# Layer 0's experts on the picked rows, and layer 1's window attention written out step by step

## The chip, the cores and the metric

The kernel runs on one core of one Trainium2 chip. The metric is the device time of one execution in microseconds (us), as the median of repeated runs. The profile is that of one execution on the same core. TensorE is PE in it (PEld its weight loads), VectorE is DVE, ScalarE is ACT, GpSimd is POOL, SyncE is SP.

## The reference

Two batches of 4096 tokens of width 256 pass through two layers, each with an attention and an expert part, in f32. The change is in layer 0's expert part and in layer 1's attention. Layer 0's expert part, cut:

```python
logits = einsum('bsd,ed->bse', x, gate_w) + gate_b      # 32 experts
probs = softmax(logits, axis=-2)                        # over the 4096 tokens
vals, idx = top_k(probs over tokens, 8)                 # each expert picks 8 tokens
tok = take_along_axis(x, idx)                           # (b, 8, 32, 256)
merged = einsum('bked,bke->bed', tok, vals)             # one row per expert
h = gelu([merged, 1] @ w1[e])                           # 257 x 1024 per expert
o = [h, 1] @ w2[e]                                      # 1025 x 256 per expert
out = zeros_like(x).at[idx].add(o * vals)               # added to the picked tokens
x = x + gb * out
```

Its input is the layer norm of x, times (1 + cb) plus sb. At most 512 of the 8192 rows of x change, and each expert's weights, 2 MB, are read for two rows (one of each batch). Layer 1's attention gives each token 16 of the scores over the 64 before it, and two more.

## The kernel before, in words

The program is a chain of stages with a barrier of all engines between them. A stage starts its semaphores, runs one instruction stream per engine and clears them. Four stages matter here.

**Token choice** (`build_token_choice`, tiles `tc_`). SP loads `x` in four chunks of 2048 tokens (2 MB each) and, behind the first, 14 small tables (identity, gate weights, modulation), on which DVE, PE and ACT wait (`consts`). DVE normalizes a chunk (`normalize`, L1634) into `h`, PE turns it and makes the logits (`turn`, `route`), ACT copies them into `probs` [32 experts, 4096 tokens] per batch. Per batch then: DVE's maximum (`peak`, L1648), ACT's exponential (L1602), and in `choose` four passes of DVE over 32x4096: the scaling (L1654), the best 8 (L1656), taking these out (L1658) and the difference (L1660), which leaves `chosen`, a dense matrix with 8 entries other than zero per expert. PE turns `chosen` (L1554) and multiplies it with `h` (L1563); `merge` makes `merged`.

**Experts** (`build_experts`, `ex_`). Eight rounds of four experts. SP loads the 4 MB of w1 and the 4 MB of w2 of a round into one of two sets of buffers; the load for round r + 2 waits for `up_done` and `down_done` of round r. PE's work in a round is `up` (L1768), the turning (L1776) and `down` (L1785), with two copies and a bias on DVE and gelu on ACT between. After the last round eight small transfers turn `outs` into `expert_out`, and L1822 adds the bias of w2.

**Scatter** (`build_scatter`, `sc_`). A loop reads all 8192 rows of `x1` again, multiplies `chosen` with `expert_out` on PE (L1883), gates (L1895) and adds (L1897) on DVE, and writes `x2`.

**Window attention** (`build_window_attention`, `wa_`). 16 steps of 512 tokens (four tiles). `run_steps` writes out the first two and the last two; the 12 between run as a hardware loop of two steps a turn, on all five engines. In a step PE and DVE work turn by turn: scores and the best 16 of a tile, probabilities, the products with the values, the sum into `x`; further on in the step DVE scales `h` of step it + 2 (`normalize`, with the modulation L2311 and L2313) and takes the values of step it + 1 (L2320). POOL makes a product of 128x1024 (L2282) and four small ones (L2288) per step.

Of the kernel before, what the change touches and what calls it, by code (L numbers as in the profile page):

```python
# [1443 lines left out]
def build_token_choice(nc, d, merged, chosen):  # L1444
# [5 lines left out]
    WAYS = P // EXPERTS  # L1450
    with ExitStack() as ctx:
        sb = lambda name, shape: ctx.enter_context(nc.sbuf_tensor("tc_" + name, shape, F32))
# [11 lines left out]
        h = sb("h", [P, GROUPS, T, DIM])  # L1464
        x = [sb(f"x{i}", [P, T, DIM]) for i in both]
# [8 lines left out]
        chosen_T = sb("chosen_T", [P, GROUPS_PER_BATCH * T, EXPERTS])  # L1474
        part = sb("part", [P, DIM])
# [3 lines left out]
        ch_ps = [ps(f"ch_ps{i}", [P, 512]) for i in both]  # L1479
        part_ps = ps("part_ps", [P, 512])  # L1480
# [3 lines left out]
        routed, logits_out, peak_ready, exp_done, chosen_ready, chosen_turned, chosen_copied, part_done, part_ready, summed, merged_out = map(sem, (  # L1484
            "routed", "logits_out", "peak_ready", "exp_done", "chosen_ready", "chosen_turned", "chosen_copied", "part_done", "part_ready", "summed", "merged_out"))
        x_in = [sem(f"x_in{i}") for i in both]
        CONSTS = 16 * (4 + BATCH + 4 * BATCH)

        sem.start()
        with nc.Block() as block:  # L1490
            @block.sync
            def _(sync):
                def load_x(g):
                    if g >= 2:
                        sync.wait_ge(h_ready, at((g - 1) * QUADS))
                    sync.dma_start(flat(x[g % 2][:, :, :]), chunk_rows(d["x1"], g)).then_inc(x_in[g % 2], 16)
# [3 lines left out]
                sync.dma_start(stack[:, :], d["stack"]).then_inc(consts, 16)  # L1500
                sync.dma_start(gate_w[:, :, :], d["gate0_wT"].rearrange("(k p) n -> p k n", p=P)).then_inc(consts, 16)
# [11 lines left out]
            def _(pe):  # L1513
# [6 lines left out]
                def turn(q, half):  # L1520
                    n = q * 2 + half
                    pe.wait_ge(h_ready, at(q + 1))
                    if n >= 2:
                        pe.wait_ge(hT_ready, at(n - 1))
                    for k in range(HALVES):
                        for t in range(2):
                            mm = pe.transpose(tr_ps[n % 2][:, (k * 2 + t) * P:(k * 2 + t + 1) * P], h[:, q // QUADS, q % QUADS * Q + half * 2 + t, k * P:(k + 1) * P], ident[:, :])
                    mm.then_inc(turned, 1)
# [18 lines left out]
                for b in range(BATCH):  # L1547
                    pe.wait_ge(chosen_ready, at(b + 1))
                    for gg in range(GROUPS_PER_BATCH):
                        n = b * GROUPS_PER_BATCH + gg  # L1550
                        if n >= 2:
                            pe.wait_ge(chosen_copied, at(n - 1))
                        for j in range(T):
                            mm = pe.transpose(ch_ps[n % 2][:, j * EXPERTS:(j + 1) * EXPERTS],  # L1554
                                              chosen[:, b, gg * P * T + j:(gg + 1) * P * T:T], ident[0:EXPERTS, 0:EXPERTS])
                        mm.then_inc(chosen_turned, 1)
                    tiles = GROUPS_PER_BATCH * T
                    pe.wait_ge(chosen_copied, at((b + 1) * GROUPS_PER_BATCH))
                    if b > 0:
                        pe.wait_ge(part_ready, at(b))  # L1560
                    for n in range(tiles):
                        way = n % WAYS
                        mm = pe.matmul(part_ps[way * EXPERTS:(way + 1) * EXPERTS, 0:DIM], chosen_T[:, n, :], h[:, b * GROUPS_PER_BATCH + n // T, n % T, :],  # L1563
                                       start=(n < WAYS), stop=(n >= tiles - WAYS), skip_group_check=True)
                    mm.then_inc(part_done, 1)

                    pe.wait_ge(part_ready, at(b + 1))
                    pe.wait_ge(weights_ready, at(1))
                    if b > 0:
                        pe.wait_ge(merged_out, at(b * HALVES))  # L1570
                    for k in range(HALVES):
                        pe.matmul(mg_ps[:, 0, k, :], part[:, k * P:(k + 1) * P], stack[:, :], start=True, stop=True, skip_group_check=True)
                        mm = pe.matmul(mg_ps[:, 1, k, :], shift[:, b, k * P:(k + 1) * P], weight_of[:, b, :], start=True, stop=True, skip_group_check=True)
                    mm.then_inc(summed, 1)

            @block.scalar
            def _(act):
                act.wait_ge(consts, at(CONSTS))
# [21 lines left out]
                def exponents(b):  # L1600
                    act.wait_ge(peak_ready, at(b + 1))
# [3 lines left out]
                for q in range(ALL_QUADS + 1):  # L1605
# [6 lines left out]
                    if q == ALL_QUADS - QUADS:  # L1612
                        exponents(0)
                exponents(1)
                for n in range(GROUPS):
                    act.wait_ge(chosen_turned, at(n + 1))
                    if n >= GROUPS_PER_BATCH:
                        act.wait_ge(part_done, at(n // GROUPS_PER_BATCH))
                    i = n % GROUPS_PER_BATCH
                    act.copy(chosen_T[:, i * T:(i + 1) * T, :].rearrange("p t e -> p (t e)"), ch_ps[n % 2][:, :]).then_inc(chosen_copied, 1)  # L1620
# [320 lines left out]
def is_first(it):  # L1941

    return isinstance(it, int) and it == 0
# [1133 lines left out]
```

## Time and profile before

| what | value |
|---|---|
| median of 3 runs | 3483.39 us (3483.12 to 3486.39) |
| profiled execution, its own time | 3495.82 us |
| its span | 3493.6 us |
| granted TensorE clock over the span | 0.77 |
| PE, DVE, ACT, POOL busy | 73%, 59%, 38%, 25% of the span |

The span is what the profile covers; 2.2 us of the execution's time lie around it. Times in rows count from the span's start. The four stages stand at these places: token choice from 1556, experts from 1694, scatter from 1875, window attention from 1967 to 2761. Behind it the slots and layer 1's experts follow, which the change doesn't touch.

### The profile page before, as it was taken

The page shows a single profiled execution, that of the slowest core. Times are in us where ns is not written, and L with a number is a line of the kernel's source. Part 1 is how long each engine was busy: PE and PEld are TensorE (multiplying, and loading weights), DVE is VectorE, ACT ScalarE, POOL GpSimd, SP SyncE. Part 2 cuts the span into 40 slices and gives each one's busy share as a digit, 9 for nine tenths or more (in the row PEclk, how much of TensorE's full clock was granted, in tenths as well). Part 3 has the DMA queues.
Part 4 walks back from the last instruction along what each step waited for, and adds up shares of the span by engine and source line. Part 5 has one row for each costly group of instructions (what it writes and reads, how often), then busy time and mean ns, then how long its engine had stood idle before and what let it go on. Part 6 is the DMA issues. An engine that isn't in the chain of part 4 may idle for free. (4 is left out here: it accounts for less than half of the span.)

```text
span 3493.6 us, 109335 instructions
## 1 busy us (share of the span) xinstructions
PE 2539.2 (73%) x42388; PEld 1878.3 (54%) x42388; DVE 2058.2 (59%) x5552; ACT 1338.1 (38%) x3189; POOL 890.0 (25%) x1201
## 2 busy tenths in 40 slices
PE   5988886358888847656576278877788348999990
PEld 2555554345555536542334255655556338999990
DVE  2387987846666635447203357777767584555557
ACT  3666674236666634424001034334444102222223
POOL 0222232115555531100000001111111005666660
PEclk8999996555555558777676589889889589999995
DMA  2457788854444445641595732212221422222218
GB/s 100 157 188 264 256 316 289 282 176 103 97 108 101 97 138 178 187 158 48 238 416 221 271 122 64 63 50 64 63 64 55 144 77 82 87 86 87 51 39 291
DMA packets 351523, 513.20 MB, mean 147 GB/s; under 512 B 119980, under 2 KB 270031, under 8 KB 345608
## 3 DMA queue, kind: packets, MB, share of 16 engines
q1 hardware_dynamic: 264616, 300.41, 26.1%
q0 software_dynamic: 67008, 175.87, 15.5%
q10 hardware_dynamic: 19744, 35.13, 2.7%
q8 instruction: 63, 1.03, 0.1%
q14 instruction: 92, 0.75, 0.1%
HBM read 319.51 MB, written 198.33 MB: 148 GB/s over the span
## 5 line engine op out<-in xcount | busy, mean ns | idle before, releaser
L1106 ACT ACTIVATE ss_write_ps<-ss_state,ss_gammas 128x64 f32<-128x64 f32 x1024 | 263.3, 303 | 195.9 <-DVE ss_state L1154 195.9
L2768 PE MATMUL se_up_ps<-se_xT,se_w 128*128 128x128 f32 x2176 | 267.7, 277 | 0.0
L477 PE MATMUL dc_rows_ps<-dc_weights,dc_hT 128*128 128x512 f32 x512 | 260.8, 634 | 6.4 <-ACT dc_rows L606 5.1
L2776 PE MATMUL se_y_ps<-se_w,se_aT 128*128 128x256 f32 x1088 | 257.2, 379 | 0.0
L2768 PEld LDWEIGHTS se_up_ps<-se_xT,se_w 128*128 128x128 f32 x2176 | 256.4, 194 | 0.1
L2833 DVE COPY se_w<-mx_weights 128x2048 f32 x136 | 167.5, 1232 | 145.0 <-issue 132.5
L2731 POOL DMA_INDIRECT scratch_picked<-se_y,se_give x136 | 200.2, 1472 | 70.5 <-issue 52.3
L1154 DVE TENSOR_TENSOR ss_state<-ss_write_ps,ss_block_mask 128x128 f32<-128x128 f32 x512 | 129.6, 291 | 135.0 <-PE ss_write_ps L1071 135.0
L1071 PE MATMUL ss_write_ps<-ss_solved,ss_k_rows 16*64 16x64 f32 x4096 | 180.6, 322 | 38.0 <-DVE ss_solved L1149 38.0
L2776 PEld LDWEIGHTS se_y_ps<-se_w,se_aT 128*128 128x128 f32 x1088 | 196.4, 190 | 21.1
L2725 POOL DMA_INDIRECT se_xs<-scratch_h,se_take x136 | 141.3, 1039 | 256.0 <-DVE se_take L2850 244.3
L1028 POOL DMA_DIRECT2D scratch_solved_u<-ss_solved x256 | 135.2, 528 | 247.8 <-DVE ss_solved L1149 225.6
L2288 POOL TENSOR_TENSOR wa_exps<-wa_exps,wa_nears 128x192 f32<-128x192 f32 x64 | 38.2, 598 | 589.1 <-ACT wa_one L2233 589.1
L1062 PE MATMUL ss_read_ps<-ss_state,ss_wq 128*32 128x64 f32 x4096 | 168.0, 314 | 26.1 <-DVE ss_state L1154 25.4
L1071 PEld LDWEIGHTS ss_write_ps<-ss_solved,ss_k_rows 16*64 16x64 f32 x4096 | 136.6, 208 | 93.7 <-ACT ss_write_ps L1106 62.0
L2808 ACT ACTIVATE se_aT<-se_up_ps 128x512 f32<-128x512 f32 x136 | 81.3, 598 | 197.4 <-PE se_up_ps L2768 197.4
L2803 ACT COPY se_xT<-se_xt_ps 128x256 f32<-128x256 f32 x136 | 50.7, 373 | 276.6 <-PE se_xt_ps L2758 276.6
L1062 PEld LDWEIGHTS ss_read_ps<-ss_state,ss_wq 128*32 128x32 f32 x4096 | 105.1, 150 | 80.3 <-DVE ss_state L1154 76.7
L1149 DVE TENSOR_TENSOR ss_solved<-ss_u_rows,ss_read_ps 128x64 f32<-128x64 f32 x512 | 107.4, 221 | 59.9 <-PE ss_read_ps L1062 51.7
L1028 POOL DMA_DIRECT2D scratch_solved_q<-ss_solved x256 | 135.2, 528 | 13.9 <-issue 10.9
L2100 PE MATMUL wa_wide_ps<-wa_hT,wa_w_cols 128*128 128x512 f32 x256 | 136.6, 684 | 0.0
L477 PEld LDWEIGHTS dc_rows_ps<-dc_weights,dc_hT 128*128 128x128 f32 x512 | 91.6, 199 | 80.6 <-issue 67.8
(364 smaller groups left out, 5655.6 us busy)
## 6 DMA issues: line engine op xcount, KB each, us to landing
ex_w<-in_w_all SPq DMA_DIRECT2D x64, 1024.0 KB, 21.0
scratch_rows<-dc_rows POOLq DMA_DIRECT2D x64, 512.0 KB, 6.1
scratch_vw<-dc_out POOLq DMA_DIRECT2D x64, 512.0 KB, 6.3
dc_c_rows<-scratch_rows SPq DMA_DIRECT2D x64, 384.0 KB, 5.7
ss_wq_rows<-scratch_vw SPq DMA_DIRECT2D x128, 128.0 KB, 2.3
scratch_picked<-wa_zeros ACTq DMA_DIRECT2D x32, 512.0 KB, 14.5
cb_y<-scratch_picked SPq DMA_DIRECT2D x32, 512.0 KB, 8.8
dc_x<-in_x SPq DMA_DIRECT2D x16, 512.0 KB, 5.2
```

Source lines behind the costliest of these rows:

```text
L477: mm = pe.matmul(to, hT[i][:, k, :], weights[:, k, columns], start=(k == 0), stop=(k == HALVES - 1), skip_group_check=True)
L1028: pool.dma_start(to, solved[i][lines, b, :, :]).then_inc(out_done[i], 16)
L1062: mm = pe.matmul(read_ps[b][u * QUAD:(u + 1) * QUAD, 0:WIDTH], wq[i][:, b, u, c, :], state[b][:, k, :], start=True, stop=True, skip_group_ ...
L1071: mm = pe.matmul(write_ps[b][side_of(u), k, 0:WIDTH], k_rows[i][rows_of(u), b, c, :], solved[i][rows_of(u), b, c, :], start=False, stop=Tr ...
L1106: ins = act.activation(write_ps[b][:, k, 0:WIDTH], state[b][:, k, :], ACT.Copy, scale=gammas[i][:, b, k, c:c + 1])
L1154: vec.tensor_tensor(state[b][:, :, :], write_ps[b][:, :, 0:WIDTH], block_mask[:, :].unsqueeze(1).broadcast_to([P, HALVES, WIDTH]), ALU.mul ...
L2100: mm = pe.matmul(bank[:, :], w_cols[:, which, k, m * P:(m + 1) * P], moving[:, k, 0:STEP], start=(k == 0), stop=(k == HALVES - 1))
L2725: pool.indirect_dma_start(xs[i % (2 * AHEAD)][:, :], None, d["h3"], bass.IndirectOffsetOnAxis(ap=take[i % (2 * AHEAD)][:, :], axis=0), bou ...
L2731: pool.indirect_dma_start(d["picked"], bass.IndirectOffsetOnAxis(ap=give[i][:, :], axis=0), y[i][:, :], None, bounds_check=PICKS * TOKENS ...
L2768: mm = pe.matmul(up_ps[i % 2][:, c * P:(c + 1) * P], w[i % (2 * AHEAD)][:, k * DFF + c * P:k * DFF + (c + 1) * P], xT[i % 2][:, k, :], sta ...
L2776: mm = pe.matmul(y_ps[i % 2][:, 0:DIM], aT[i % 2][:, c, :], w[i % (2 * AHEAD)][:, HALVES * DFF + c * DIM:HALVES * DFF + (c + 1) * DIM], st ...
L2833: vec.tensor_copy(w[i % (2 * AHEAD)][:, :], weights[:, bass.ds(expert, 1), :].rearrange("p a f -> p (a f)")).then_inc(w_ready, 1)
```

## The change

Token choice keeps no `h` and no `chosen`. DVE normalizes a chunk in place, in a ring of three buffers. After all four chunks `choose(b)` takes the best 8 logits (`max`) and their places (`max_index`), and ACT's exponential runs for the sum and for the best 8 alone. Small matmuls of PE spread places and shares over 128 partitions (`unstack`, `ones`), POOL gathers the 2 x 128 picked rows per batch from `x1` by indirect transfers, DVE normalizes those alone, and PE merges them. ACT issues the eight loads of round 0's weights (8 MB) on its own queue at the start of token choice and waits for them at its end.

In the expert stage DVE builds `weight_at`, the shares of all experts for each picked row (`add_hits`, in rounds 0 to 3), and the places to store to, each row once (`write_once`). After the rounds four matmuls give what each picked row gets, DVE gates and adds it, and POOL stores the rows into `x1` by four indirect transfers. The scatter stage is gone, and `x2` with it.

In the window attention all 16 steps are written out on ACT, POOL and DVE (`write_steps` for `run_steps`; PE and SP keep the loop), and the two modulations of `h` go from DVE to POOL (`modulate`).

The diff, cut to its core:

```diff
@@ build_token_choice, SP, PE
                 load_x(0)
                 sync.dma_start(ident[:, :], d["ident"]).then_inc(consts, 16)
                 sync.dma_start(stack[:, :], d["stack"]).then_inc(consts, 16)
+                sync.dma_start(unstack[:, :], d["unstack"]).then_inc(consts, 16)
+                sync.dma_start(ones[:, :], d["ones_square"][0:EXPERTS, :]).then_inc(consts, 16)
+                sync.dma_start(own_pick[:, :], d["own_pick"]).then_inc(consts, 16)
...
+                spread_places(0)
+                spread_shares(0)
+                spread_places(1)
+                merge(0)
+                spread_shares(1)
+                merge(1)
+            @block.gpsimd
...
+                        pool.indirect_dma_start(rows[:, b * 2 + n, :], None, d["x1"], bass.IndirectOffsetOnAxis(ap=where[b * 2 + n][:, :], axis=0),
...
             @block.scalar
             def _(act):
+                for j in range(SET):
+                    act.dma_start(w1[0][j][:, :, :], d["w1_all"][j, 0:DIM, :].rearrange("(k p) n -> p k n", p=P)).then_inc(w1_in[0], 16)
+                for j in range(SET):
+                    act.dma_start(w2[0][j][:, :, :], d["w2_all"][j, 0:HIDDEN, :].rearrange("(p c) n -> p c n", p=P)).then_inc(w2_in[0], 16)
                 act.wait_ge(consts, at(CONSTS))
...
-                    if q == ALL_QUADS - QUADS:
-                        exponents(0)
+                exponents(0)
                 exponents(1)
+                root(GROUPS)
+                root(GROUPS + 1)
...
+                act.wait_ge(w1_in[0], 16 * SET)
+                act.wait_ge(w2_in[0], 16 * SET)
@@ build_token_choice, DVE
+                    seq.done(vec.max(top[:, b, :], probs[:, b, :]))
...
+                    seq.tell(vec.max_index(top_at[:, b, :], top[:, b, :], probs[:, b, :]), found, b + 1)
...
-                    seq.done(vec.tensor_scalar(probs[:, b, :], probs[:, b, :], stat[:, b, 2:3], None, ALU.mult))
-                    seq.done(vec.max(top[:, b, :], probs[:, b, :]))
-                    seq.done(vec.match_replace(chosen[:, b, :], top[:, b, :], probs[:, b, :], 0.0))
-                    seq.tell(vec.tensor_tensor(chosen[:, b, :], probs[:, b, :], chosen[:, b, :], ALU.subtract), chosen_ready, b + 1)
...
-                for g in range(GROUPS - 1):
+                for g in range(GROUPS):
                     normalize(g)
-                peak(0)
-                normalize(GROUPS - 1)
                 choose(0)
-                peak(1)
+                find_rows(0)
+                share(0)
                 choose(1)
+                find_rows(1)
+                own_shares(0)
+                measure_rows(0)
+                normalize_rows(0)
+                share(1)
+                own_shares(1)
                 merge(0)
+                measure_rows(1)
+                normalize_rows(1)
                 merge(1)
@@ build_experts
+        CONSTS = 16 * (4 + BATCH)
...
-                pe.wait_ge(consts, at(48))
+                pe.wait_ge(consts, at(CONSTS))
...
+                pe.wait_ge(finished, at(BATCH))
...
+                        mm = pe.matmul(o_ps[b][:, n * DIM:(n + 1) * DIM], weight_at[:, b, n * P:(n + 1) * P], expert_out[:, b, :], start=True, stop=True, skip_group_check=True)
...
+                        pool.indirect_dma_start(d["x1"], bass.IndirectOffsetOnAxis(ap=to[b * 2 + n][:, :], axis=0), rows[:, b * 2 + n, :], None,
...
+                    if r < BATCH * TOP // QUAD:
+                        for n in range(r * QUAD, (r + 1) * QUAD):
+                            add_hits(n)
+                    if r == BATCH * TOP // QUAD:
+                        write_once()
...
-def build_scatter(nc, d, chosen, expert_out):
@@ build_window_attention
+def write_steps(step):
+    for it in range(ALL_STEPS):
+        step(it, it % 2, it // 2, it + 1 < ALL_STEPS, it + 2 < ALL_STEPS)
...
+                def modulate(it, i):
+                    pool.wait_ge(h_scaled, at(it + 1))
+                    pool.tensor_tensor(h[i][:, :, :], h[i][:, :, :], mod[i][:, 1:2, :].broadcast_to([P, NT, DIM]), ALU.mult).then_inc(h_weighed, 1)
+                    pool.wait_ge(h_weighed, at(it + 1))
+                    pool.tensor_tensor(h[i][:, :, :], h[i][:, :, :], mod[i][:, 0:1, :].broadcast_to([P, NT, DIM]), ALU.add).then_inc(h_ready, 1)
...
-                    seq.done(vec.tensor_tensor(h[i][:, :, :], h[i][:, :, :], mod[i][:, 1:2, :].broadcast_to([P, NT, DIM]), ALU.mult))
-                    seq.wait()
-                    seq.tell(vec.tensor_tensor(h[i][:, :, :], h[i][:, :, :], mod[i][:, 0:1, :].broadcast_to([P, NT, DIM]), ALU.add), h_ready, it + 1)
+                    vec.sem_inc(h_scaled, 1)
...
-                run_steps(vec, step)
+                write_steps(step)
```

The order of SP's transfers at the start of the expert stage, before the change (`ex_w_0_0` to `ex_w_0_3` are the buffers of round 0, first w1's rows, then w2's; `ex_members` and the two `ex_w_bias` are the tables that PE and DVE wait for):

```order
L1729 DMA ex_w_0_0<-in_w_all 128x2x1024
L1729 DMA ex_w_0_1<-in_w_all 128x2x1024
L1729 DMA ex_w_0_2<-in_w_all 128x2x1024
L1729 DMA ex_w_0_3<-in_w_all 128x2x1024
L1736 DMA ex_members<-in_members 128x8
L1737 DMA ex_w_bias<-in_w_bias 128x256
L1738 DMA ex_w_bias<-in_w_all 32x256
L1733 DMA ex_w_0_0<-in_w_all 128x2048
```

And the same place in the changed program (here `ex_w_0` to `ex_w_3` are the buffers of round 1, and `w_first`, further down, those of round 0, used again for round 2):

```order
L1809 DMA ex_members<-in_members 128x8
L1810 DMA ex_w_bias<-in_w_bias 128x256
L1811 DMA ex_w_bias<-in_w_all 32x256
L1803 DMA ex_w_0<-in_w_all 128x2x1024
...
L1807 DMA ex_w_3<-in_w_all 128x2048
L1814 DMA ex_earlier<-in_earlier 128x512
L1816 DMA ex_gb<-scratch_mod 128x256 x2
L1803 DMA w_first<-in_w_all 128x2x1024 x4
```

Round 0's loads are gone from here (ACT issues them a stage earlier), and of the six tables that PE and DVE now wait for, three stand behind round 1's 8 MB.

POOL in the window attention, before, from the stage's start into the loop:

```order
L2276 MEMSET wa_zeros 128x1024
L2282 ISA
L2282 TENSOR_TENSOR wa_pT<-wa_qT,wa_pT 128x1024
L2288 TENSOR_TENSOR wa_exps<-wa_exps,wa_nears 128x192 x4
L2282 TENSOR_TENSOR wa_pT<-wa_qT,wa_pT 128x1024
L2288 TENSOR_TENSOR wa_exps<-wa_exps,wa_nears 128x192 x4
L2282 TENSOR_TENSOR wa_pT<-wa_qT,wa_pT 128x1024
L1934 UNCONDITIONAL_BRANCH
```

And after:

```order
L2339 MEMSET wa_zeros 128x1024
L2350 ISA
L2350 TENSOR_TENSOR wa_h<-wa_h,wa_mod 128x1024
L2352 TENSOR_TENSOR wa_h<-wa_h,wa_mod 128x1024
L2350 TENSOR_TENSOR wa_h<-wa_h,wa_mod 128x1024
L2352 TENSOR_TENSOR wa_h<-wa_h,wa_mod 128x1024
L2345 TENSOR_TENSOR wa_pT<-wa_qT,wa_pT 128x1024
L2358 TENSOR_TENSOR wa_exps<-wa_exps,wa_nears 128x192 x4
L2345 TENSOR_TENSOR wa_pT<-wa_qT,wa_pT 128x1024
L2350 TENSOR_TENSOR wa_h<-wa_h,wa_mod 128x1024
L2352 TENSOR_TENSOR wa_h<-wa_h,wa_mod 128x1024
```

The loop's branch is gone, and each step gets the two modulations behind its product; two pairs stand ahead of the first product.

## Rows read from the trace of the kernel before

**Rows 1.** stage windows; us, busy us (count) per engine, PE clock, DMA share, GB/s.

```profile
1556.00:1694.00 138.00, 77.47 (x408) 38.38 (x408) 90.96 (x191) 44.48 (x61) 0.00 (x0) 0.72 0.17 63
...
1694.00:1875.00 181.00, 117.60 (x896) 63.39 (x896) 18.41 (x28) 3.73 (x11) 0.00 (x0) 0.75 0.92 373
...
1875.00:1967.00 92.00, 56.79 (x128) 41.17 (x128) 44.07 (x64) 8.62 (x8) 0.00 (x0) 0.50 0.48 188
...
2047.00:2761.00 714.00, 558.59 (x2477) 411.31 (x2476) 506.88 (x1735) 281.80 (x558) 73.46 (x79) 0.88 0.18 56
```

**Rows 2.** timeline of DVE in token choice; start us, busy us, instructions, [idle <-releaser].

```profile
1566.88 0.68 DVE L1628 TENSOR_SCALAR tc_scaled_w<-tc_gate_w,tc_mod_T 128x32 f32<-128x32 f32 x4 [19.36 <-DMA tc_shift<-scratch_mod]
...
1567.95 5.32 DVE L196 BATCH_NORM_STATS2 tc_stats<-tc_x 128x6 f32<-128x256 f32 x16 [0.22 <-DVE tc_bias L1630]
...
1599.79 5.26 DVE L1642 TENSOR_SCALAR tc_h<-tc_x,tc_moments,tc_scale_shift 128x256 f32<-128x256 f32 x16
...
1638.69 4.42 DVE L1656 MAX8 tc_top<-tc_probs 32x8 f32<-32x4096 f32 x1
...
1692.08 0.41 DVE L1676 SCALAR_TENSOR_TENSOR merged<-tc_mg_ps,tc_mod_T,tc_outer 128x32 f32<-128x32 f32 x2
```

**Rows 3.** groups of instructions in token choice.

```profile
L1537 PE MATMUL tc_lg_ps<-tc_hT,tc_scaled_w 128*32 128x512 f32 x64 | 36.0, 694 | 0.0
...
L1527 PE MATMUL tc_tr_ps<-tc_ident,tc_h 128*128 128x128 f32 x128 | 20.6, 313 | 23.6 <-ACT tc_hT L1590 14.6 <-DVE tc_h L1642 9.0
...
L1602 ACT ACTIVATE tc_probs<-tc_probs,tc_stat 32x4096 f32<-32x4096 f32 x2 | 7.4, 3707 | 9.7 <-DVE tc_stat L1648 9.7
...
L1602 ACT ACT_TABLE_LOAD x1 | 1.3, 1283 | 0.0
```

**Rows 4.** DMA queues: SP's at token choice's start; both where ACT shares (2774:2791).

```profile
q1 hardware_dynamic: 2031, 2.79, 76.5%
...
q10 hardware_dynamic: 2595, 3.46, 60.6%
q1 hardware_dynamic: 2598, 2.63, 46.9%
```

**Rows 5.** timeline in the expert stage: first weight issue, PE's rounds, DVE's end.

```profile
1694.82 2.22 SPq L1729 DMA_DIRECT2D ex_w<-in_w_all  x3
...
1708.26 5.66 PE L1768 MATMUL ex_rows_ps<-ex_w,ex_picked 128*32 128x512 f32 x32 [16.48 <-DMA ex_w_bias<-in_w_all]
...
1850.77 3.64 PE L1768 MATMUL ex_rows_ps<-ex_w,ex_picked 128*32 128x512 f32 x32 [3.47 <-DMA ex_w<-in_w_all]
...
1874.10 0.75 DVE L1822 TENSOR_TENSOR expert_out<-expert_out,ex_w_bias 32x256 f32<-32x256 f32 x2 [6.67 <-DMA expert_out<-ex_outs]
```

**Rows 6.** indirect transfers of layer 1, one line each.

```profile
DMA to landing us min/median/max: 2.7/2.8/4.1
...
L2731 POOL DMA_INDIRECT scratch_picked<-se_y,se_give x136: 977/1444/2034, 2904.6 to 3406.4; - x136
```

**Rows 7.** a step of the window attention: DVE modulation, PE value products.

```profile
L2313 DVE TENSOR_TENSOR wa_h<-wa_h,wa_mod x16: 1224/1224/1226, 2019.7 to 2664.8; 128x1024 f32<-128x1024 f32 x16
...
2297.59 1.03 PE L2108 MATMUL wa_v_ps<-wa_w_rows,wa_phT 128*128 128x256 f32 x4
...
2301.66 1.13 PE L2108 MATMUL wa_tr_ps<-wa_w_rows,wa_hT 128*128 128x256 f32 x4 [3.04 <-DVE wa_v L2320]
...
2305.77 1.29 PE L2108 MATMUL wa_v_ps<-wa_w_rows,wa_phT 128*128 128x256 f32 x4
```

**Rows 8.** DVE at L2352: idle by releaser; its first row after the loop.

```profile
  issue: 22.6, 6
...
2633.84 0.36 DVE L2352 SCALAR_TENSOR_TENSOR wa_scores<-wa_sc_ps,wa_band 128x192 f32<-128x192 f32 x1
```

**Rows 9.** POOL and DVE operations on SBUF alone, durations min/median/max.

```profile
L2282 POOL TENSOR_TENSOR wa_pT<-wa_qT,wa_pT x16: 2343/2348/2357, 2040.5 to 2702.6; 128x1024 f32<-128x1024 f32 x16
...
L2392 DVE SCALAR_TENSOR_TENSOR wa_out<-wa_out,wa_one,wa_ga x64: 484/485/2024, 2061.9 to 2746.1; 128x256 f32<-128x256 f32 x64
```

More of the change, by code:

```diff
@@ L1449, in build_token_choice @@
     ALL_QUADS = GROUPS * QUADS
-    WAYS = P // EXPERTS
+    RING = 3
+    places, shares, where, rows, row_places = (pick[n] for n in ("places", "shares", "where", "rows", "row_places"))
     with ExitStack() as ctx:
-        sb = lambda name, shape: ctx.enter_context(nc.sbuf_tensor("tc_" + name, shape, F32))
+        sb = lambda name, shape, dt=F32: ctx.enter_context(nc.sbuf_tensor("tc_" + name, shape, dt))
         ps = lambda name, shape: ctx.enter_context(nc.psum_tensor("tc_" + name, shape, F32))
@@ L1463, in build_token_choice @@
         bias = sb("bias", [EXPERTS, BATCH])
-        h = sb("h", [P, GROUPS, T, DIM])
-        x = [sb(f"x{i}", [P, T, DIM]) for i in both]
+        unstack = sb("unstack", [EXPERTS, P])
+        ones = sb("ones", [EXPERTS, P])
+        own_pick = sb("own_pick", [P, TOP])
+        x = [sb(f"x{i}", [P, T, DIM]) for i in range(RING)]
         stats = sb("stats", [P, T, 6])
@@ L1478, in build_token_choice @@
         lg_ps = [ps(f"lg_ps{i}", [EXPERTS, 512]) for i in both]
-        ch_ps = [ps(f"ch_ps{i}", [P, 512]) for i in both]
-        part_ps = ps("part_ps", [P, 512])
+        places_ps = ps("places_ps", [P, BATCH, TOP * EXPERTS])
+        own_ps = [ps(f"own_ps{n}", [P, BATCH, TOP]) for n in range(2)]
         mg_ps = ps("mg_ps", [P, 2, HALVES, EXPERTS])
@@ L1545, in _, with spread_places, spread_shares, merge @@
                         route(q - 1)
[L1547 to L1568, printed above, removed]
+                def spread_places(b):
+                    pe.wait_ge(spread_ready, at(b + 1))
+                    pe.matmul(own_ps[0][:, b, :], unstack[:, :], places[:, b, :], start=True, stop=True, skip_group_check=True).then_inc(places_done, 1)
+                    pe.matmul(places_ps[:, b, :], ones[:, :], on_diagonal[:, b, :, :].rearrange("e k f -> e (k f)"), start=True, stop=True, skip_group_check=True).then_inc(places_done, 1)
+                def spread_shares(b):
+                    pe.wait_ge(shares_ready, at(b + 1))
+                    pe.matmul(own_ps[1][:, b, :], unstack[:, :], shares[:, b, :], start=True, stop=True, skip_group_check=True).then_inc(shares_done, 1)
+                def merge(b):
+                    pe.wait_ge(normed_ready, at(b + 1))
                     if b > 0:
@@ L1701, in build_experts @@
         members = sb("members", [P, MEMBERS])
-        w1 = [[sb(f"w1_{s}_{j}", [P, HALVES, HIDDEN]) for j in range(SET)] for s in both]
-        w2 = [[sb(f"w2_{s}_{j}", [P, HC, DIM]) for j in range(SET)] for s in both]
+        w1 = [w1[0], [sb(f"w1_{j}", [P, HALVES, HIDDEN]) for j in range(SET)]]
+        w2 = [w2[0], [sb(f"w2_{j}", [P, HC, DIM]) for j in range(SET)]]
+        gb = sb("gb", [P, BATCH, DIM])
+        hit = [sb(f"hit{i}", [EXPERTS, PICKED]) for i in both]
+        earlier = sb("earlier", [P, 2, PICKED])
+        same = sb("same", [P, PICKED])
+        repeats = sb("repeats", [P, BATCH, 2])
+        to_f = sb("to_f", [P, BATCH, 2])
+        to = [sb(f"to{n}", [P, 1], INT) for n in range(2 * BATCH)]
+        weight_at = sb("weight_at", [EXPERTS, BATCH, PICKED])
+        added = sb("added", [P, BATCH, 2, DIM])
         w1_bias = sb("w1_bias", [P, EXPERTS, HC])
@@ L1900 @@
+                for b in range(BATCH):
+                    vec.wait_ge(added_up, at(b + 1))
+                    vec.tensor_tensor(added[:, b, :, :], o_ps[b][:, :].rearrange("p (n f) -> p n f", n=2), gb[:, b:b + 1, :].broadcast_to([P, 2, DIM]), ALU.mult).then_inc(gated, 1)
+                    vec.wait_ge(gated, at(b + 1))
+                    vec.tensor_tensor(rows[:, b * 2:b * 2 + 2, :], rows[:, b * 2:b * 2 + 2, :], added[:, b, :, :], ALU.add).then_inc(rows_ready_to_go, 1)
 WINDOW, TOPK, PHRASE = 64, 16, 32
```

279 lines of the change are left out of this document (152 added, 127 removed).

## Prediction

> **What bounds the kernel now.** I read the table of stage windows first, then each of the four stages by the timeline of the engine that ends last in it. The windows [rows 1] show four stages with different limits. Token choice (138 us): PE and DVE are both busy little more than half the time, so its end is a chain, not an engine. Experts (181 us): the DMA engines are busy 0.92 of it, DVE hardly at all; the weights bound it. Scatter (92 us): no engine is busy much above half, the DMA share is 0.48, and all of it is on the path, since barriers stand on both sides. Window attention (714 us): PE 559 and DVE 507 busy, which work turn by turn, so what DVE spends ahead of PE's next input counts in full. The change touches 1125 us of 3493.6.
>
> **Token choice.** DVE's first operation starts at 1566.88, having waited for the last small table [rows 2]. Call the start of the first normalization N0 = 1567.95. The third one ends at 1599.79 + 5.26 = 1605.05, so one takes 12.4 us. The stage's last sum ends at 1692.49 [rows 2] and the next stage's first load leaves at 1694.82 [rows 5], N0 + 126.9: a barrier costs 2.3.
>
> After the change, from the same N0: four normalizations, 49.5. The best 8 of batch 0, one pass of 4.42 [rows 2]; max_index stands in no row at this width, so I bound it by half a pass (2.3) and two passes (8.8) and take one, 4.4, since it reads the same 4096 elements. That makes N0 + 59. PE needs 36.0 + 20.6 us for turning and logits [rows 3], the first rows are ready 7 us after N0, and the last copy follows 1 us later: N0 + 64.6. Behind that ACT takes 1.28 for the table and 3.7 for the exponential: N0 + 69.5, and DVE, which waits there in order, goes on to the second batch's two passes (N0 + 78.9), ACT's exponential (N0 + 83). What is left is two batches of small steps (spreading shares, a root, normalizing two tiles, six small matmuls, merging): by the pieces of before, 16 us; I bound it by 10 and 22. With the barrier's 2.3 that is N0 + 101.3, 25.6 us earlier. The gathers by POOL start in time: four, 1.0 to 2.0 us each, landing 2.8 after their start [rows 6], beside the second batch's passes.
>
> N0 itself moves. ACT issues eight loads of 1 MB at the stage's start, while SP's first chunk and 17 tables come. Where both queues are full [rows 4], q10 and q1 moved 2595 and 2598 packets in the same stretch: they take turns packet by packet, whatever the packets' size. SP's share at this stage's start was 2031 packets, mostly small; the loads are about 1536 packets of 4 and 8 KB. So nearly all of the 8.39 MB go by ahead of SP's last table: 2.1 + 8.39 + 0.35 MB at 412 GB/s (8.39 MB in a round of 20.4 us, [rows 5]: (1850.77 - 1708.26)/7) are 26.3 us, some 28.4 with issue and landing. Before, the tables were there 10.9 us after the stage's window opens at 1556. N0 comes 17.5 us later. Bounds: 2 us (three more tables at the 0.7 us which 15 transfers took each) and 20 (all of 8.39 MB). I take 17.5, since [rows 4] is the same pair of queues. Here the Trainium skill, DMA: Bandwidth & Descriptors, section "Queues, rings and completion order", says that each DMA engine goes round between the queues with work, a whole packet at a time. The equal counts of packets agree; the rule speaks against the early loads being free, and gives the same 17.5.
>
> Token choice thus gains 25.6 - 17.5 = 8.1 us; the next stage starts at S = 1686.7.
>
> **Experts.** Before, PE's first matmul came 13.4 us after the first load, waiting for tables behind 4 MB. After, round 0's weights are there, but PE and DVE wait for six tables, of which three stand behind round 1's 8 MB: 9.1 MB at 412 GB/s and the 2.9 us of start that 13.4 us leaves over 4.36 MB, S + 25. So the early loads don't start PE earlier here, but 12 us later; what they save is 8.39 MB of the stage's traffic, 20.4 us. Round 0's up ends at S + 30; the next w1 then streams alone, DMA stands still in part, and from down's end (S + 41.6, by the 16.6 us of PE's chain: 117.6/8 busy [rows 1] and some 2 of copies and gelu between) 11 half rounds of 10.2 us follow: S + 155.8 with 2 us of landing. Eight chains of 16.6 from S + 25 end at S + 158, so PE is nearly a second bound. Before, 67.3 MB and the start take 166.3 us by the same rate, and the stage's last sum ends at 1874.85 [rows 5], 180.0 after its first load, thus 13.7 behind. After: S + 169.5. DVE's added work (30 small passes, 4 sums over 256) lies in rounds where it was busy 18 us of 181 [rows 1].
>
> The tail is new: four matmuls (0.5 each), two gates and two adds (0.7 each, half hidden), four indirect stores on POOL at 1.44 [rows 6] and about 3 to land: 11 us, bounds 8 and 16. With a barrier of 2.3 the window attention starts at S + 182.8 = 1869.5 instead of 1967: **97.5 us** gained, of which the scatter stage alone is 92 and its new tail takes 11 back.
>
> **Window attention.** Three terms. (1) The two modulations leave DVE: 2 x 1.22 us [rows 7], in 14 of 16 steps ahead of the values that PE waits for (3.04 at 2301.66): 34.3. POOL has them done 5 us after DVE's scaling at its own 2.35 each [rows 9], and PE turns that `h` only in the next step, so the longer operation is hidden there; in the prologue it isn't, -2.4. (2) DVE's loop turns: 22.6 us of "issue" in 6 waits at L2352, the first instruction of a step [rows 8], and PE waits behind them. Written out, nearly all of it goes: 22.3. PE keeps its loop, and shows no such wait at its turn today. (3) After PE's wait of 3.04, its value products run slower at first, as at TensorE's lower level of 1.2 GHz: 16 of them from 2301.66 to 2307.06, 5.4 us, where the upper level, 2.4 GHz, makes at most 4.1 (four such rows at the 1.03 of 2297.59). With a wait of 0.6 left the clock may hold: 1.3 x 14 = 18; I take two thirds, 12. Sum 34.3 + 22.3 - 2.4 + 12 = **66 us**, bounds 54 and 72.
>
> **Sum.** 97.5 + 66 = 163.5 of the profile's 3495.8 (span 3493.6 and 2.2 around it), so 3332 there. The median lies 12.4 us, 0.36%, lower; I take the saving as the same on it: 3483.4 - 163.5 = **3320 us**.
>
> **Rivals.** (a) The early loads don't hold up the tables, if SP's transfers are served first because they are issued first: N0 moves by 2 only, and the time is 3304. For: SP issues its tables while ACT issues the loads, so some are there first. Against: [rows 4]. (b) POOL's modulations and DVE's operations on two SBUF inputs shut each other out. L2392, which sums two rows of SBUF, takes 0.485 at the median and 2.024 at most [rows 9], and the long one lies beside a running L2282 on POOL. If each step lost one whole POOL operation, 14 x 2.35 = 33 us, the time is 3353. Against: by then DVE is at L2320, which reads PSUM and shows no such spread. The Trainium skill, SBUF — State Buffer, section "Who interferes with whom", calls this an exclusive lock for a whole instruction, which the single long L2392 agrees with; by that rule alone the loss is what (b) says. (c) PE's clock gives nothing back, and the small steps in token choice and the tail take their upper bounds: 12 + 6 + 5, 3343. (d) The other side: written out, DVE's code is read from memory as it runs, and each refill could stop it as a loop turn does, some 4 us each [rows 8]. Slower than before needs 164 us more, some 40 refills, over two per step, in place of the turns. Against: 2633.84 [rows 8] is the first row after the loop, in code that runs straight on, and there is no wait before it. (e) Nothing comes of it, if token choice's small steps grow by as much as the rest gives: 164 us there are over seven times their upper bound of 22. The time would be 3483.
>
> **How the numbers follow.** Forecast as summed: 0.52; (a) 0.15; (b) 0.12; (c) 0.16; (d) 0.03; (e) and anything else 0.02. The range takes in (a), (b) and both bounds of the attention: from 3304, less 6 for the attention and 6 and 3 for the small steps' and the tail's lower bounds, to (b): 3290 to 3354. A measurement here tells 0.2%, 7 us, from no change; all cases but (d) and (e) lie far below 3476. Faster 0.95, same 0.01, slower 0.04.
>
> **What would show it.** Token choice: DVE's first row comes about 28 us after SP's first issue; under (a) about 12. Experts: PE's first up waits for `ex_gb` or `ex_earlier` until S + 25, and the stage with its stores lasts some 181 us. Window attention: no L2352 row with a wait of 4 us for issue, a step of about 40 us where 714/16 = 44.6 stands now, POOL's new rows at 2.35. What would make me wrong: small steps in token choice that wait for each other far more than 16 us; L2392 rows of 2 us in most steps; indirect stores of many us.

## The result and the profile after

The changed kernel takes **3367.77 us** (median of 4 runs, 3364.82 to 3369.65) against 3484.01 before; the ratio is 0.966 (95% interval 0.9648 to 0.9672). It is faster by 116 us, where the prediction had 163.5 and 3320, and its range ended at 3354. The direction was right, the size was not, and the time lies 14 us outside the range.

The profiled execution took 3364.82 us (span 3363.1). The tables below count a stage from SP's first load in it to SP's first load in the next one, so that a run's other stages don't enter. That matters here: the profiled spans differ by 130.5 us, not 116, since that of before was taken 11.8 us above its median and reached token choice 8.8 us later than the changed kernel, in code that is the same in both.

| stage | before | forecast | after |
|---|---|---|---|
| token choice | 138.4 | 130.3 | 131.1 |
| experts and scatter | 272.3 | 182.8 | 186.7 |
| window attention | 796.6 | 730.6 | 769.4 |

So token choice and the experts came out within 5 us of the working, and the window attention missed it by 39: of 66 us it gave 27.

Stage windows of the kernel after, with columns as in [rows 1]; the third lies at the place in the attention that answers to the last of [rows 1]:

```profile
1547.00:1678.00 131.00, 60.48 (x236) 30.15 (x236) 77.52 (x231) 44.89 (x63) 4.12 (x4) 0.68 0.35 134
...
1678.00:1865.00 187.00, 114.79 (x904) 65.44 (x904) 34.51 (x76) 3.73 (x11) 3.95 (x4) 0.70 0.80 322
...
1947.00:2635.00 688.00, 549.43 (x2469) 402.22 (x2467) 501.91 (x1707) 282.03 (x558) 141.42 (x107) 0.90 0.19 58
```

DVE's busy time in the attention fell from 507 us to 502 only, though two operations of 1.22 us left it in each step, and POOL's doubled, from 73 to 141. So DVE got something back. The groups (durations in ns, min/median/max) and the timeline of the same stretch, DVE and POOL, show what. The copy in the kernel before stands first:

```profile
L2316 DVE COPY wa_v<-wa_v x16: 282/285/286, 2027.6 to 2706.0; 128x256 f32<-128x256 f32 x16
...
L2388 DVE COPY wa_v<-wa_v x16: 282/2481/2483, 1923.8 to 2576.9; 128x256 f32<-128x256 f32 x16
...
L2350 POOL TENSOR_TENSOR wa_h<-wa_h,wa_mod x16: 2339/2342/2343, 1916.5 to 2534.7; 128x1024 f32<-128x1024 f32 x16
...
2188.51 1.38 DVE L220 TENSOR_SCALAR wa_h<-wa_h,wa_moments,wa_scale_shift 128x256 f32<-128x256 f32 x4
...
2190.03 2.48 DVE L2388 COPY wa_v<-wa_v 128x256 f32<-128x256 f32 x1
...
2192.55 0.69 DVE L2392 TENSOR_TENSOR wa_v<-wa_tr_ps,wa_row_bias 128x512 f32<-128x512 f32 x1
...
2190.02 2.34 POOL L2350 TENSOR_TENSOR wa_h<-wa_h,wa_mod 128x1024 f32<-128x1024 f32 x1 [2.76 <-DVEq L2385]
...
2192.44 2.35 POOL L2352 TENSOR_TENSOR wa_h<-wa_h,wa_mod 128x1024 f32<-128x1024 f32 x1
```

DVE ends the scaling of `h` and tells POOL; POOL starts its multiplication at 2190.02, and DVE's next instruction is the copy of the carried values (L2388, which was L2316 and took 0.28 us in each of its 16 executions before). It starts at 2190.03 and ends at 2192.51, 0.15 us behind POOL's operation. It does so in 15 of its 16 executions; the one short copy, 0.282, is the last, behind which there is nothing to modulate. The first two of the four sums at L2392 (L2320 before) run beside POOL's second operation at their usual 0.69. And PE still waits for these sums, and still runs slower behind the wait (last line: the window of these products, columns as in [rows 1]):

```profile
2193.29 1.13 PE L2171 MATMUL wa_tr_ps<-wa_w_rows,wa_hT 128*128 128x256 f32 x4 [2.85 <-DVE wa_v L2392]
...
2195.66 1.91 PE L2171 MATMUL wa_v_ps<-wa_w_rows,wa_hT 128*128 128x256 f32 x4
...
2197.36 1.34 PE L2171 MATMUL wa_v_ps<-wa_w_rows,wa_phT 128*128 128x256 f32 x4
...
2193.29:2198.70 5.41, 5.41 (x17) 4.49 (x18) 1.24 (x2) 0.00 (x0) 1.50 (x1) 0.68 0.00 0
```

It waits 2.85 us where it waited 3.04 in [rows 7], and the 16 products take 5.4 us as before, at a granted clock of 0.68. Not every step shows this: in four of 14 the products take 3.7 us after the same wait, at a clock of 1.00 (before, in three of 14).

### The profile page after: what moved, and what is told of

Read it like the earlier page. It is cut to its first block and busy times, and to the rows that moved or that the text cites. A ratio compares the mean times of both kernels' runs of the same rounds, so it can differ in the third digit from the quotient of the medians.

```text
span 3363.1 us, 107724 instructions
## 1 busy us (share of the span) xinstructions
PE 2446.5 (73%) x42096; PEld 1818.5 (54%) x42096; DVE 2012.8 (60%) x5544; ACT 1330.3 (40%) x3183; POOL 974.7 (29%) x1241
## 3 DMA queue, kind: packets, MB, share of 16 engines
q1 hardware_dynamic: 261896, 275.28, 25.4%
## 5 line engine op out<-in xcount | busy, mean ns | idle before, releaser
L1028 POOL DMA_DIRECT2D scratch_solved_q<-ss_solved x256 | 135.9, 531 | 13.2 <-issue 10.9
```

Source lines behind the costliest of these rows:

```text
L1028: pool.dma_start(to, solved[i][lines, b, :, :]).then_inc(out_done[i], 16)
```

## The experiments

Ratios are to the kernel before, run beside each on the same chip; the changed kernel's is 0.966. The attention's length is the number to look at in the first three. A stage's length is that of one profiled execution; runs that share a stage's code agree in it within 0.2 us in token choice (130.9 to 131.1), within 4 us in the experts (186.3 to 189.7) and within 3 us in the attention (767.2 to 769.7).

**The copy ahead of POOL.** Nothing is moved between engines; only the signal to POOL stands one instruction later.

```diff
-                def normalize(seq, it, i):
+                def normalize(seq, it, i, tell=True):
...
                     seq.wait()
-                    vec.sem_inc(h_scaled, 1)
+                    if tell:
+                        vec.sem_inc(h_scaled, 1)
...
                     seq.done(vec.tensor_copy(v[i][:, 0, 0:DIM], v[1 - i][:, NT, 0:DIM]))
                     seq.wait()
+                    if tell:
+                        vec.sem_inc(h_scaled, 1)
...
-                        normalize(seq, it + 2, n)
+                        normalize(seq, it + 2, n, tell=False)
...
-                        take_values(seq, it + 1, 1 - n)
+                        take_values(seq, it + 1, 1 - n, tell=norm)
```

> The changed kernel, but DVE tells POOL that h is scaled only behind its copy of the last values (L2388), so POOL's modulation can't start ahead of that copy. Theory (the copy waits for a whole POOL operation, 2.48 us in place of 0.28, 15 times): the copy takes 0.28 again, 33 us go, about 3335 us; if PE also keeps its upper clock in the value products, up to 18 more, 3317. Rival (the copy's 2.48 us only fill time in which PE is behind anyway): the copy is short, and DVE waits for PE instead, 3362 to 3368.

Measured: 3319.51 us, ratio 0.951 (0.9494 to 0.9526); the attention takes 719.1 us, 50.3 less than in the changed kernel. The copy's group, and the timeline of DVE, POOL and PE in a step of this run:

```profile
L2389 DVE COPY wa_v<-wa_v x16: 285/295/2503, 1926.4 to 2533.0; 128x256 f32<-128x256 f32 x16
...
2176.23 0.29 DVE L2389 COPY wa_v<-wa_v 128x256 f32<-128x256 f32 x1
...
2179.45 0.69 DVE L2395 TENSOR_TENSOR wa_v<-wa_tr_ps,wa_row_bias 128x512 f32<-128x512 f32 x1 [1.49 <-PE wa_tr_ps L2171]
...
2176.66 2.36 POOL L2350 TENSOR_TENSOR wa_h<-wa_h,wa_mod 128x1024 f32<-128x1024 f32 x1 [3.09 <-DVEq L2392]
...
2177.41 1.13 PE L2171 MATMUL wa_tr_ps<-wa_w_rows,wa_hT 128*128 128x256 f32 x4 [0.67 <-DVE wa_v L2395]
...
2180.11 1.03 PE L2171 MATMUL wa_v_ps<-wa_w_rows,wa_phT 128*128 128x256 f32 x4
...
2177.41:2181.14 3.73, 3.73 (x17) 3.31 (x18) 1.24 (x2) 0.00 (x0) 3.65 (x2) 1.00 0.01 2
```

The copy takes 0.29 us, POOL starts behind it, and the four sums beside POOL's two operations are not held up. One copy is still long, 2.50 us: the first, ahead of step 0, where the signal still stands before it. PE waits 0.67 us in place of 2.85, and its 16 products take 3.7 us (2177.41 to 2181.14) in place of 5.4: the granted clock is 1.00, the upper level. So they do in all 14 steps. The copies account for 14 x 2.2 = 31 us and the products, which were slow in ten steps, for 10 x 1.7 = 17, together 48 of the 50. The theory holds and the rival falls.

**The modulations back on DVE.** The two operations return to `normalize`, `modulate` goes from POOL, the steps stay written out.

```diff
-                    vec.sem_inc(h_scaled, 1)
+                    seq.done(vec.tensor_tensor(h[i][:, :, :], h[i][:, :, :], mod[i][:, 1:2, :].broadcast_to([P, NT, DIM]), ALU.mult))
+                    seq.wait()
+                    seq.tell(vec.tensor_tensor(h[i][:, :, :], h[i][:, :, :], mod[i][:, 0:1, :].broadcast_to([P, NT, DIM]), ALU.add), h_ready, it + 1)
```

> The changed kernel with the two modulations of h back on DVE; the steps stay written out. Theory (what the move takes off DVE, 2.45 us a step, the wait of the copy gives back, 2.2): the same time to 4 us, 3364 to 3372, the copy at 0.28. Rival (the move did save its 34 us and the shortfall lies elsewhere): 3400.

Measured: 3363.75 us, 0.964 (0.9623 to 0.9656); the attention takes 769.7 us, against 769.4, and the copy is short again in all its executions:

```profile
L2385 DVE COPY wa_v<-wa_v x16: 283/285/288, 1925.7 to 2576.9; 128x256 f32<-128x256 f32 x16
```

So the move to POOL was worth nothing as it stands in the changed kernel, as the theory had it.

**The loop back.** ACT, POOL and DVE run the steps as a hardware loop again, POOL keeps the modulations.

```diff
-                write_steps(step)
+                run_steps(vec, step)
```

> The changed kernel with the hardware loop back in the window attention on ACT, POOL and DVE; the modulations stay on POOL. Theory (the turns of DVE's loop cost 4 us each on the path): 22 us more, 3390, with the waits for issue back at the first scores of a turn. Rival (they were hidden, and what the attention gained has another cause): 3368 to 3373.

Measured: 3371.75 us, 0.9664 (0.9644 to 0.9685); the attention takes 774.2 us, 4.8 more. That is the rival's time, and the theory's waits aren't there. Waits of DVE for "issue" (for nothing that the trace shows) at this line, in this run: us in total, times, longest:

```profile
DVE wa_scores L2424 <- issue: 3.3, 6, 0.6
```

3.3 us in six waits, 0.6 at the longest, where [rows 8] has 22.6 in six. Something else than writing out the steps has taken these waits away. Seven more kernels looked for it.

**The attention wholly as it was,** loop and modulations on DVE, behind the changed experts (both edits above together):

> The changed kernel with the window attention as it was before: hardware loop and modulations on DVE; the experts stay changed. Theory (the turns of DVE's loop stall when the modulations stand in its body, as before): waits of 4 us at the first scores of a turn, 22 us more than with the steps written out, 3386. Rival (whether a turn stalls depends on where in memory the loop has come to lie, which the change of the stages ahead has moved): no such waits, 3364 to 3372.

Measured: 3384.55 us, 0.9704 (0.9686 to 0.9722); the attention takes 780.3 us, 16 less than before with the same code. Waits of DVE, and the queues that carry instructions, in 500 us of the loop (packets, MB, share):

```profile
DVE wa_scores L2421 <- issue: 2.9, 6, 0.5
...
q8 instruction: 3, 0.05, 0.0%
...
q14 instruction: 5, 0.04, 0.0%
```

The waits are 0.5 us at most, and in these 500 us eight packets of instructions were fetched, the last at 2094.5. The time is that of the first expectation (3386), but the trace is that of the second: no waits of 4 us. The trace is of the fastest of the four executions, 3375.26 us; what the other three, 7 to 14 us longer, waited for wasn't traced. A body with the same instructions doesn't stall in it, so the theory as stated falls. Of the 10.6 us that the attention takes over the run with its steps written out and the modulations on DVE, DVE was idle for 7.4 and busy for 3.1, in small pieces.

**The kernel before, its attention written out** and nothing else changed:

> The kernel before, with the window attention's 16 steps written out on ACT, POOL and DVE, and nothing else changed; the modulations stay on DVE. Theory (the waits at the turns of DVE's loop are on the path before the change): no wait of 4 us at the first scores of a step, the attention 22 us shorter, 0.6% below the kernel before. Rival (they are hidden behind PE): within 0.1% of the kernel before.

Measured: 3452.02 us, 0.9892 (0.9875 to 0.9908); the attention takes 766.9 us, 30 less. So in the kernel before, the waits at the turns were on the path. That the gain is more than their own 22.6 us doesn't show that they cost more: in the changed kernel, whose turns don't stall, writing out still gives 4.8 (or 10.6 with the modulations on DVE: 780.3 against 769.7).

**The code moved.** Three kernels before with 32, 96 and 192 fills that do nothing, ahead of the attention's loop on DVE:

```diff
+                for n in range(32):
+                    vec.memset(unused[:, n:n + 1], 0.0)
```

> The kernel before, loop and all, with 32 tiny fills of an unused tile on DVE at the start of the window attention, which do nothing but move the code behind them on by 32 instructions. Theory (whether a turn stalls depends on where the loop lies in memory; with the changed experts it lay 30 instructions further on and didn't stall): the waits at the turns fall from 4.4 to about 0.5 us, instruction fetches stop after the first turns, and the time is 0.5 to 0.6% below the kernel before. Rival (the stall belongs to something else that the changed experts removed): 22 us of waits as before, the time of the kernel before.

> As the run with 32 fills, but 96 of them. Theory (placement): waits and fetches come and go together, whichever it is here. Rival (not placement): waits of 4 us at the turns, as before.

> The kernel before, loop and all, with 192 tiny fills of an unused tile on DVE at the start of the window attention. With 0, 32 and 96 the turns stalled. Theory (placement, with a loop of 379 instructions that stalls when it lies badly against blocks of code that are fetched as a whole; a bad stretch that holds 0, 32 and 96 need not hold 192): the waits at the turns fall from 4.8 to about 0.5 us and the fetches stop after the first turns; the time is 10 to 22 us below the kernel before, as the fills themselves may lengthen the start of the stage. Rival (not placement): 24 us of waits at the turns, as with the other pads, the time of the kernel before or up to 10 us more.

Measured: 3491.66 (1.0006, 0.9995 to 1.0017), 3489.23 (one run), 3485.06 (0.9988, 0.9977 to 1.0). The waits stay in all three, 24.1, 24.1 and 22.0 us. In the run with 192:

```profile
DVE wa_scores L2355 <- issue: 22.0, 6, 4.7
...
q14 instruction: 28, 0.23, 0.1%
```

28 packets on this queue in 500 us of the loop, about five for each turn, where the loop behind the changed experts had five in all. (The trace doesn't say for which engine a packet is.) Waits and fetches go together in every run whose attention is a loop, but moving DVE's code by these amounts governs neither. And fetches alone don't make DVE wait: with the steps written out, the changed kernel has 17 packets on the same queue in 500 us and 0.3 us of such waits in the whole stage.

**The scatter's loop written out, and the scatter left out,** both in the kernel before:

> The kernel before, with the scatter's hardware loop (two turns) written out; the attention keeps its loop and the modulations on DVE. Theory (the attention's loop stalls at its turns when another loop of the same engines stands in the program ahead of it, one stage before): no waits over 1 us at the first scores of a turn, instruction fetches stop after the first turns, the attention some 22 us shorter. Rival (the scatter's loop has nothing to do with it): waits of 4 to 5 us as before.

> The kernel before without its scatter stage, which leaves out the addition of the experts' result to x; the attention reads x1. It prices the stage alone. Theory (the stage is wholly on the path): 90 to 92 us less than the kernel before. As to the turns of the attention's loop: if the stage's presence decides, its waits fall to 0.5 us and it is 112 to 120 us less; if it is token choice's or the experts' code, the waits stay at 4 to 5 us.

Measured: 3494.18 (one run), waits 24.0 us; and 3401.71, ratio 0.9746 (0.9721 to 0.977), waits 23.8. The scatter isn't what decides on the waits. Its own price is clear now: from token choice's start to the attention's 322.6 us pass without it, and 410.7 with it: 88.

**The tables of the experts ahead of round 1's weights:**

```diff
-                load_w1(1)
-                load_w2(1)
                 sync.dma_start(earlier[:, :, :], d["earlier"]).then_inc(consts, 16)
                 for b in range(BATCH):
                     sync.dma_start(gb[:, b, :], mod_row(d, 0, b * GROUPS_PER_BATCH, MOD_GB)).then_inc(consts, 16)
+                load_w1(1)
+                load_w2(1)
```

> The changed kernel, but SP issues the tables earlier and gb ahead of round 1's weights in the expert stage. Theory (PE starts 25 us late because it waits for tables behind 8 MB, while round 0's weights lie ready): PE's first matmul comes about 5 us after the stage's first issue in place of 25.4, DMA doesn't stand still, and the stage ends 10 to 12 us earlier, 3357. Rival (the stage is bound by its weights' traffic, whenever PE starts): PE starts early and waits in round 2, 3365 to 3368.

Measured: 3363.18 us, 0.9636 (0.962 to 0.9652); the stage takes 179.9 us in place of 186.7. PE's first row in the stage, in the changed kernel and then in this run:

```profile
1704.15 6.46 PE L1843 MATMUL ex_rows_ps<-w_first,ex_picked 128*32 128x512 f32 x32 [28.63 <-DMA ex_gb<-scratch_mod]
```

```profile
1687.71 4.94 PE L1843 MATMUL ex_rows_ps<-w_first,ex_picked 128*32 128x512 f32 x32 [11.70 <-DMA ex_gb<-scratch_mod]
```

PE starts 8.5 us after the stage's first load in place of 25.4, and the stage gains 6.8, not 10 to 12: from the fourth round on PE waits for weights, as the rival had it from round 2 on. The time lies between the two expectations.

**ACT's loads behind the tables of token choice:** the eight loads and the wait for `consts` change places.

```diff
+                act.wait_ge(consts, at(CONSTS))
                 for j in range(SET):
                     act.dma_start(w1[0][j][:, :, :], d["w1_all"][j, 0:DIM, :].rearrange("(k p) n -> p k n", p=P)).then_inc(w1_in[0], 16)
...
-                act.wait_ge(consts, at(CONSTS))
```

> The changed kernel, but ACT issues its eight loads of round 0's weights behind its wait for the tables of token choice. Theory (the loads and the tables take turns by packets, so the loads hold up the first normalization by 17.5 us): DVE's first row comes 13 to 14 us after the stage's first issue in place of 30.9, the rest of the stage is as it was, 3351. Rival (the loads then hold up the second and third chunk of x instead): the gaps before the second and third normalization grow, and 8 us or less are left of the gain, 3360 or more.

Measured: 3351.22 us, 0.9603 (0.958 to 0.9625); token choice takes 115.8 us in place of 131.1. Queues at the stage's start in the changed kernel, DVE's first row in it, and then two rows of DVE in this run:

```profile
q10 hardware_dynamic: 1664, 8.39, 65.3%
...
q1 hardware_dynamic: 2311, 3.48, 32.4%
...
1578.57 0.68 DVE L1654 TENSOR_SCALAR tc_scaled_w<-tc_gate_w,tc_mod_T 128x32 f32<-128x32 f32 x4 [39.95 <-DMA tc_shift<-scratch_mod]
```

```profile
1560.10 0.68 DVE L1654 TENSOR_SCALAR tc_scaled_w<-tc_gate_w,tc_mod_T 128x32 f32<-128x32 f32 x4 [19.93 <-DMA tc_shift<-scratch_mod]
...
1572.76 0.25 DVE L1666 RECIPROCAL tc_scale_shift<-tc_scale_shift 128x16 f32<-128x16 f32 x1 [5.14 <-ACT tc_scale_shift L1608]
```

In the changed kernel 1664 packets of ACT's queue, all 8.39 MB, had gone by when DVE could start, 30.9 us after the stage's first load; in this run it starts after 10.9. Of these 20 us the stage keeps 15.3. ACT issues the eight loads from 1560.10 to 1572.46, 12.3 us, and only then takes the root that the first normalization waits for, so DVE waits 5.1 us there (second row). The second and third normalization have no such gap, so the rival falls.

**No early loads at all:** SP loads round 0's weights in the expert stage, w1, then the six tables, then w2.

> The changed kernel without early loads: SP loads round 0's weights in the expert stage, w1, then all six tables, then w2. Theory (the early loads take 17.5 us in token choice and save less in the experts, where PE waits for tables anyway): token choice 17 us shorter, PE's first matmul 15 us after the stage's first issue, the stage 9 us longer, 3360. Rival (the early loads save the whole 20 us of their traffic in the experts): 3371.

Measured: 3357.6 us, 0.9618 (0.9601 to 0.9635). Token choice takes 112.2 us and the experts 198.1, together 310.3 against 317.8 in the changed kernel and 305.5 with the late loads. But those two have the experts' tables behind round 1's weights, and this run doesn't, so the 7.5 and 4.8 us aren't the loads' alone. Runs with the tables ahead tell more: with the early loads as in the change, the two stages take 131.0 and 179.9, 310.9 together (the run before last), and with the loads behind the tables of token choice 296.5 (the next run). As they stand in the change, the loads cost 18.9 us in token choice and save 18.2 in the experts, so they are worth nothing; issued behind the tables, they save 14.

**The three edits together:**

> The changed kernel with three edits: DVE's copy ahead of POOL's modulation, the expert stage's tables ahead of round 1's weights, ACT's loads behind the tables of token choice. Theory (the three costs lie in three stages and add up: 50, 7 and 17 us): 3294. Rival (the late loads of weights aren't there when the experts start, so that the second and third edit cost each other): PE's first matmul waits for the first weights, 3300 to 3312.

Measured: **3294.81 us**, 0.9451 (0.9429 to 0.9474), against an expectation of 3294. Stages: 115.8, 180.7 and 717.8 us. PE's first matmul in the experts comes 8.5 us after the stage's first load, as with the tables first alone, so the rival falls. The costs lay in three stages and add up, and this kernel beats both.

## Why the prediction was off

**The step that failed** is the first term of the window attention: "POOL has them done 5 us after DVE's scaling at its own 2.35 each, and PE turns that `h` only in the next step, so the longer operation is hidden there". For PE it is hidden. For DVE it isn't: the first thing that DVE does after telling POOL is a copy that doesn't run beside POOL's operation. The term was 34.3 us and measured none (769.7 us without the move, 769.4 with it): 15 copies, each 2.2 us longer, took back 33. Rival (b) had an exclusion like it, at 33 us in the attention, but named operations with two inputs in SBUF, as `out`'s gating had shown a collision in [rows 9]; the copy has one. That the price fits is partly luck. I set the rival aside with "by then DVE is at L2320", and so passed over the one instruction between the scaling and L2320, the copy of 0.28 us. The Trainium skill, SBUF — State Buffer, section "SBUF: two separate sides", names both kinds: besides operations on two SBUF inputs those in which DVE uses two ports, with a copy of f32 in SBUF as the example, and says that the one which comes second waits for the whole instruction. The trace agrees for the copy: 2.48 us beside 2.34, and 0.28 alone. That the sums of the values, with one input in PSUM, are not held up agrees as well.

**The third term,** PE's clock, fell with the first: 12 us forecast, none measured, as the wait of 2.85 us stayed. In the run with the copy first both terms come: from 769.7, with the modulations on DVE, to 719.1 they are worth 50.6, where the forecast had 34.3 - 2.4 + 12 = 43.9. The 6.7 more are the third term's: the products were slow in 11 of 14 steps before, not in all, but the fast ones take 3.7 us, not 4.1, so that 11 x 1.7 = 19 us come back and not 12.

**The second term,** the loop's turns, had about the right size for the changed kernel (the waits are gone; without the move to POOL the attention gained 26.9 us, 796.6 to 769.7, for 22.3 forecast), but by luck, not for the reason given. Writing out the steps removes the waits in the kernel before (30 us of the attention there), yet with the changed stages ahead of it the loop has no such waits either: 16 of the 26.9 us come without writing anything out. Which part of the change does that stays open: not the scatter's presence, not its loop, not a move of DVE's code by 32, 96 or 192 instructions. The changed code of token choice and of the experts is what remains of the change, and no run took either alone.

**Token choice** came out at 131.1 for 130.3. DVE's first operation came 30.9 us after the stage's first load, forecast 28.4, and from the first normalization on the stage took 99.1 us, forecast 101.3: two misses that cancel. `max_index` took 4.41 at both places, one pass, as chosen. Rival (a) is out: SP's tables were not served first, 1664 packets of ACT's queue going by beside 2311 of SP's before the last table was there.

**The experts** took 186.7 for 182.8: PE's start at 25.4 (25 forecast), the last sum at 171.1 (169.5), and a tail with barrier of 15.6 (13.3); POOL's four stores took about 1 us each, 0.3 apart. The scatter's 92 us were, alone, 88. The early loads cost 18.9 us in token choice (forecast 17.5) and, once the tables stood ahead of round 1's weights, saved 18.2 in the experts (forecast 20.4).

**Rivals (d) and (e)** did not come. The first rows of all steps together wait 0.3 us for issue in the changed kernel, whose steps run straight on, though instructions are fetched all along (17 packets in 500 us).

## What to carry to other kernels

Before an operation goes to POOL, list what DVE does next and look at every instruction of it, the short ones first: a copy of 0.28 us became one of 2.48, 15 times, and gave back nearly all that the move took off DVE. One signal placed behind that copy was worth 50 us. Loads that are issued early on a second queue are not free while small tables on the first are waited for: here the same loads were worth nothing ahead of the tables and 14 us behind them. And the engine that issues them is busy with it: eight loads held ACT for 12.3 us.

## What the runs showed of the hardware that was not expected

Beside a loop of two steps on DVE, with the same instructions in its body, instructions were fetched at each turn in one program (28 packets on q14 in 500 us, and 4 to 5 us of waiting at each turn) and not in another (5 packets, waits of 0.5 us). Moving that code by 32, 96 or 192 instructions changed neither. The same steps written out fetched 17 packets in 500 us, with waits of 0.3 us in all.

After a wait of 0.67 us (2.09 in the first step) PE's products took 3.7 us for 16 in every step, at a granted clock of 1.00 in the one shown. After 2.85 us (4.27 in the first) they took 5.4 in ten steps of 14 (0.68 in the one shown, with single groups of four at 1.60 and 1.91 us in place of 1.03) and 3.7 in the other four, at 1.00.
